# Three edits to an attention and expert-routing kernel: registers read a block ahead, gate steps spread, turned keys written at once

## What is computed

```python
xn = layernorm(x)
# attention: 16 heads of 128 + 64 rotary columns, latents of 128
c_Q, c_KV = xn @ W_DQ.T, xn @ W_DKV.T
k_R = rope(xn @ W_KR.T)                      # 64 columns, one for all heads
scores = clip(q @ k.T, -80, 80), causal; attn = softmax(scores / sqrt(192)) @ v
# experts: a shared one for every token, and the best 3 of 7 by a biased gate
p = softmax(xn @ gate_w + gate_b); chosen = top_k(p + biases, 3)
ffn(x, w1, wg, w2) = (silu(x @ w1) * (x @ wg)) @ w2
out = x + attention(xn) + ffn(xn, shared) + sum_e share_e * ffn(xn, expert e)
```

## Time and profile before

| | before |
|---|---|
| median of 3 runs | 1353.98 us (1353.33 to 1354.11) |
| the profiled execution's own time | 1354.13 us |
| its span, first to last instruction | 1352.40 us |
| TensorE products / weight loads | 97% / 80% of the span |
| VectorE / ScalarE / GpSimd | 55% / 46% / 47% |
| mean granted clock of TensorE | 0.997 |

### The profile page before, as it was taken

The page is one execution under the profiler, slowest core; times in us unless marked ns, Lnnn a source line. Parts: engine busy times, 40 slices in busy tenths (PEclk is TensorE's granted clock), DMA queues, the critical chain, the costliest instruction groups (busy, mean ns, idle before and its releaser), DMA issues.

```text
span 1352.4 us, 21141 instructions
## 1 busy us (share of the span) xinstructions
PE 1313.1 (97%) x6553; PEld 1085.1 (80%) x6553; DVE 741.2 (55%) x1365; ACT 620.2 (46%) x1146; POOL 629.5 (47%) x534
## 2 busy tenths in 40 slices
PE   5999999999999999999998999999999999999998
PEld 3778888778888888888886788888888888888887
DVE  6361165232222222222224678888888888788876
ACT  6421143222222222222225566666676667667664
POOL 5125584994060003200001476677666776676553
PEclk9999999999999999999999899999999999999999
DMA  8125552664241213311115124323242323322012
GB/s 274 54 106 199 191 182 77 184 185 133 64 148 56 63 53 105 108 50 62 59 37 179 39 46 79 76 44 82 39 92 46 72 62 64 76 40 61 17 47 95
DMA packets 72953, 123.25 MB, mean 91 GB/s; under 512 B 10960, under 2 KB 19280, under 8 KB 72848
## 3 DMA queue, kind: packets, MB, share of 16 engines
q1 hardware_dynamic: 42000, 60.49, 15.5%
q0 software_dynamic: 11312, 27.23, 9.3%
q10 hardware_dynamic: 19536, 34.17, 7.7%
HBM read 74.41 MB, written 39.05 MB: 84 GB/s over the span
## 4 chain that ended last, share of the span: by engine, by line
PE 88%; POOL 6%; DVE 2%; issue 1%; DMA 1%; ACT 1%; POOLq 0%; SPq 0%; ACTq 0%; DVEq 0%
PE bank L48 79%; PE bank L1648 4%; POOL slots L523 3%; PE bank L1440 2%; POOL slots L521 2%; PE bank L1381 1%; PE bank L1557 1%; DMA rows_b<-in_x 1%; PE bank L1367 0%; DMA rot_sin<-sum_b 0%; POOL slots L467 0%; DVE stats L886 0%; PE bank L1501 0%; POOL store_a L529 0%; POOLq L523 0%
## 5 line engine op out<-in xcount | busy, mean ns | idle before, releaser
L48 PE MATMUL bank<-store_b,store_a 128*128 128x512 f32 (+1 forms) x1536 | 324.6, 363 | 6.7 <-DVE store_b L1249 3.2
L48 PE MATMUL bank<-slots,x_turned 128*128 x1296 | 324.2, 399 | 6.1 <-POOL slots L523 3.9
L48 PEld LDWEIGHTS bank<-store_b,store_a 128*128 128x128 f32 x1536 | 255.0, 190 | 60.3 <-issue 8.7
L48 PEld LDWEIGHTS bank<-slots,x_turned 128*128 128x128 f32 x1296 | 235.8, 188 | 66.9 <-issue 22.9
L932 DVE TENSOR_TENSOR hid_t<-bank,hid_t 128x512 fp32r<-128x512 f32 x70 | 48.4, 691 | 357.7 <-ACT hid_t L651 357.7
L48 PE MATMUL bank<-slots,hid_t 128*128 (+1 forms) x840 | 208.6, 397 | 3.4 <-DVE hid_t L932 3.4
L48 PEld LDWEIGHTS bank<-slots,hid_t 128*128 128x128 f32 x840 | 153.5, 188 | 34.8 <-DVE hid_t L932 2.1
L48 PE MATMUL bank<-store_b 128*128 128x512 f32 x768 | 179.4, 389 | 0.0
L48 PEld LDWEIGHTS bank<-store_b 128*128 128x128 f32 x768 | 144.1, 188 | 29.9
L521 POOL CAST slots<-staging 128x512 f32 (+1 forms) x84 | 51.5, 613 | 182.0 <-PE bank L48 180.2
L825 ACT ACTIVATE p_store<-bank 128x512 f32<-128x512 f32 x160 | 95.6, 598 | 85.9 <-PE bank L48 84.4
(11 more groups left out here) (204 smaller groups left out, 1825.3 us busy)
## 6 DMA issues: line engine op xcount, KB each, us to landing
staging<-in_w SPq DMA_DIRECT2D x56, 256.0 KB, 2.8
sorted_y<-y_store ACTq DMA_DIRECT2D x54, 256.0 KB
rows<-sorted_x ACTq DMA_DIRECT2D x51, 260.0 KB, 2.7
rot_sin<-sum_b SPq DMA_DIRECT2D x128, 64.0 KB, 2.0
staging<-in_wg SPq DMA_DIRECT2D x28, 256.0 KB, 2.8
shared_y<-y_store ACTq DMA_DIRECT2D x16, 256.0 KB
raw<-in_wot SPq DMA_DIRECT2D x16, 256.0 KB, 2.8
acc<-in_x SPq DMA_DIRECT2D x16, 256.0 KB, 5.4
```

The lines of the kernel that those rows point to most:

```text
L48: made = pe.matmul(out, a, b, start=first and n == 0, stop=last and n == len(pairs) - 1, skip_group_check=onto)
```

## The change

The registers of a routed block are read by a function of its own, `find_job`. For block 16 it is called behind the projections and ahead of `up`; for the others in the block before, behind the row transposes and ahead of `down`. The wait on `job_low` stays in `up`. The 16 last steps of the gate are drawn in three portions (six after block 5's `multiply`, five before block 6's, the rest after it) and not all after block 5's. The two additions of the turned keys become one with twice the columns, whose inputs are read twice by a broadcast.

```diff
@@ projections, VectorE @@
-                dve.tensor_tensor(kr[:, i, 0, :], kr_cos[:, i, :], kr_sin[:, i, :], ALU.add)
-                dve.tensor_tensor(kr[:, i, 1, :], kr_cos[:, i, :], kr_sin[:, i, :], ALU.add).then_inc(on["kr_done"], 1)
+                cosine, sine = (v[:, i, :].unsqueeze(1).broadcast_to([P, 2, DR]) for v in (kr_cos, kr_sin))
+                dve.tensor_tensor(kr[:, i], cosine, sine, ALU.add).then_inc(on["kr_done"], 1)
@@ block loop, VectorE @@
-                if b in (4, 5):
-                    for _ in range(3 if b == 4 else 10):
+                if b in (4, 5, 6):
+                    for _ in range({4: 3, 5: 10, 6: 5}[b]):
                         next(gate, None)
                 multiply(b)
...
                 if b == 5:
+                    for _ in range(6):
+                        next(gate, None)
+                if b == 6:
                     for _ in gate:
                         pass
@@ TensorE @@
-            def job_ready(b):
+            def find_job(b):
...
-                made = pe.value_load(block_tab[0:1, r, 0:1], min_val=CH, max_val=CH * NE)
+                made_by[b] = pe.value_load(block_tab[0:1, r, 0:1], min_val=CH, max_val=CH * NE)
                 at_slot[b] = nc.values_load(block_tab[0:1, r, 1:2], engines=PE_ONLY, min_val=0, max_val=SLOT,
                                             skip_runtime_bounds_check_because="made on the chip from comparisons")
-                pe.wait_ge(on["job_low"], made)
...
@@ up @@
-                    job_ready(b)
+                    pe.wait_ge(on["job_low"], made_by[b])
@@ block loop, TensorE @@
                 if b == NT:
                     projections()
+                    find_job(NT)
                 up(b)
...
                 if NT + 1 < b + 1 < NBK:
                     turn_block(b + 1 - NT)
+                if NT <= b < NBK - 1:
+                    find_job(b + 1)
                 if b and b != NT:
                     down(b - 1)
```

More of the change, by code:

```diff
@@ L1389, in tokens @@
                 return x_turned[b % 2][:, 0], x_turned[b % 2][:, 1]
-            at_slot = {}
+            at_slot, made_by = {}, {}
             def weights(b, k):
```

## The result

| | before | changed |
|---|---|---|
| median | 1353.65 us | 1335.88 us (1334.69 to 1336.61) |
| ratio | | 0.9866, interval 0.9851 to 0.9881 |
| span of the profiled execution | 1352.40 us | 1334.80 us |

A forecast was written before the change was run, and what follows sets the result against it. TensorE, busy for 97% of the span, was taken as the bound, with time won only where it stands still. Savings of 6.2 + 1.2 + 0.7 + 5.2 + 1.9 + 1.2 = 16.4 us gave 1337.7 us, range 1334.2 to 1343.0.

The forecast's parts named there:

- Ordinary blocks: Blocks 26 to 69: gap before `up` closes, period 9.272 to 9.12 us; 6.2 us saved, bounds 4.5 and 6.5.
- The discount of 0.3 us for longer gaps: Ordinary blocks: 6.2 taken, not 6.5 us; some gaps (0.36 us and more) weren't explained by the register loads' duration alone.
- The place ahead of `down`: Moved register work ahead of `down(b-1)` costs nothing, as the sequencer is there 3.2 us before `down`.
- Blocks 16 and 17: Block 16's `up` starts 0.29 us behind L910, 1.2 us saved; the gap before block 17's `up` goes, 0.7 us.
- Blocks 18 to 25: Gaps where GpSimd holds L918 shrink, 0.1 to 0.2 us left in six; 5.2 us saved, bounds 3.0 and 5.8.
- Rival 1: Meetings with GpSimd fall badly in projections and blocks 18 to 25, savings there 0 and 3.0: 1341.1 us; chance 0.14.
- The gate's steps: `hid_low(5)` runs earlier, so TensorE's 2.07 us gap before `down(5)` goes; 1.9 us saved, bounds 1.7 and 1.9.
- Turned keys: Projections: one addition is held once by GpSimd where two are held twice; 1.2 us saved, bounds 0 and 2.8.
- rival 4: Attention's clock: the 16 us shift moves, drops or doubles a fall costing 3.4 us, 1334.3 or 1341.1 us; chance 0.10.
- Rival 2: L910's semaphore and travel, not register work, end last before `up`; the 6.2 us stay unsaved: 1346.5 us; chance 0.05.
- rival 5: The sequencer's lead is otherwise used, so only the gate's and keys' parts are saved: 1351.0 us; chance 0.03.
- rival 3: Register loads before `down` stop the sequencer until TensorE's queue is empty, 1.0 us in 53 blocks: 1390.7 us; chance 0.03.

The follow-up runs named there:

- registers alone: Kernel before with only `find_job` and its calls, gate steps and key additions as before: 1338.92 us, ratio 0.9887.
- behind down: Changed kernel with the registers of block b+1 read behind `down(b-1)`, directly ahead of `up(b+1)`: 1336.14 us, ratio 0.9864.
- new place twice: Changed kernel with added register work in `find_job` (loads written twice, 1.6 us of work in all): 1337.74 us, ratio 0.9878.
- after scale behind: Changed kernel with `row_low` ahead of `scale` in all three places: 1335.44 us, ratio 0.9858.
- Keys alone: Kernel before with only the one addition in place of two for the turned keys: 1353.35 us, ratio 0.9995.
- split late: Kernel before with GpSimd's first split of expert weights put behind the projections' turns: 1374.29 us, one run.
- gate alone: Kernel before with only the gate's last steps spread over two blocks: 1352.88 us, ratio 0.9987.
- scale behind: Kernel before with VectorE's two `scale` operations put behind the low half L910 in routed blocks from 18 on: 1349.17 us, ratio 0.9966.
- new place six: Changed kernel with five more rounds of register loads written into `find_job` (seven loads a block ran, 4.2 us): 1403.5 us, one run.

## Why the prediction was right, point by point

**Ordinary blocks** (6.2 us, measured 7.23 from block 26 to 69). The mechanism is shown: 0.65 us of added work costs its full length at the old place and nothing at the new one. The period came out at 391.49 / 43 = 9.104 us where the sum had 9.12. Four kernels with the work moved (registers alone, behind down, new place twice, after scale behind) have the same 391.49: with no wait left, the stage takes exactly what is queued. 7.23 us is more than the upper bound of 6.5, since 43 periods shorter by 0.016 us are 0.7 us. The discount of 0.3 us for longer gaps was wrong as well. They came mainly from a pause between the second load and the next sequencer entry, 0.09 to 0.21 us in every second block and 0.06 in the others; it is hidden with the rest. Keys alone and split late have the same pauses, nearly all in the same blocks and of the same length, gate alone and scale behind have none. What makes them no run shows.

**The place ahead of `down`** (nothing). Right; its limit, a lead of about 3.2 us, was measured as 3.3.

**Blocks 16 and 17** (1.2 and 0.7 us, measured 1.41 and 0.91). For 1.41: from the last turn's weight load to that of block 16 it was 2.09 us and is 0.68. I had priced the way from L910's end to the first weight load at 0.29 us, from the 0.25 us behind the second register load. It is less:

```profile
307.68 1.22 DVE L918 TENSOR_TENSOR row_share<-rows,owner 128x8 f32<-128x8 f32 x1
...
309.01 0.68 DVE L910 TENSOR_TENSOR x_turned<-bank,x_turned 128x512 fp32r<-128x512 f32 x1
309.83 1.77 PEld L48 LDWEIGHTS bank<-slots,x_turned 128*128 128x128 f32 x8
```

L910 ends at 309.69 and `up` of block 27 loads at 309.83, 0.14 us later. The other waits of `up` can be taken while the sequencer stands waiting, and then only one address step is left. Block 16 has 0.13 us as well.

**Blocks 18 to 25** (5.2 us, measured 5.98). The same rows show the worst meeting with GpSimd in the changed kernel: L918 held for 1.22 us and yet no gap. The 0.1 to 0.2 us that I left in six such gaps were that mis-sized 0.29. Rival 1 fell for this stage: the meetings go on, they only no longer reach TensorE. For the projections it was live, as gate alone showed (3.2 us of idle time instead of 2.8).

**The gate's steps** (1.9 us, measured 2.0: the 1.70 us up to block 15 and 0.28 by which the first product of this execution came later; 1.9 in gate alone). In the changed kernel, VectorE and `down(5)`, each in order of time:

```profile
92.19 0.69 DVE L932 TENSOR_TENSOR hid_t<-bank,hid_t 128x512 fp32r<-128x512 f32 x1 [2.15 <-ACT hid_t L651]
92.79 0.19 DVE L1138 CAST job_tab<-small 128x7 int32<-128x7 f32 x1
95.80 0.68 DVE L927 TENSOR_TENSOR hidden<-bank,hidden 128x512 f32<-128x512 f32 x1
...
98.23 0.36 DVE L1170 CAST block_tab<-block_f 128x54 int32<-128x54 f32 x1
...
93.83 2.68 PEld L48 LDWEIGHTS bank<-slots,hid_t 128*128 128x128 f32 x12
```

`hid_low(5)` ran at 92.19 and no longer at 94.88; it now waits for ScalarE and not for the gate, and `down(5)` has no idle time before it. The last step ends at 98.6 against a forecast of 98.4, and GpSimd begins to split at 178.0, sooner than before, so the later tables cost nothing:

```profile
L521 POOL CAST slots<-staging x84: 604/612/723, 178.0 to 533.0; 128x512 f32 x72, 128x512 fp32r<-128x512 f32 x12
```

**Turned keys** (1.2 us, measured 1.8, which is the 3.17 us saved from block 15 to 16 less block 16's 1.41). The additions and the turns behind them:

```profile
L948 DVE TENSOR_TENSOR kr<-kr_cos,kr_sin x16: 291/294/1115, 177.8 to 213.7; 128x128 f32<-128x128 f32 x16
L1503 PEld LDWEIGHTS bank<-ident,c 128*128 128x128 f32 x15 | 2.1, 140 | 1.1 <-issue 1.1
```

One addition takes 0.29 us alone and up to 1.12 us held; the idle time falls from 2.8 to 1.1 us. I took little because the meetings shift; in the seven profiles with the single addition the idle time was 1.0 to 1.6 us. The Trainium skill (SBUF — State Buffer, who interferes with whom) lets a VectorE instruction with two SBUF inputs contend with a GpSimd instruction that reads SBUF, and the later of the two waits; by that a tile with one addition can be held once and not twice. The trace agrees. Before, nine of the 32 additions were held, in seven of the tiles, and in two tiles both of the pair. Now seven of the 16 are, one of them by only 0.04 us. But five of the seven tiles had a single hold before too. Beyond the additions' own time the holds fell from 5.3 to 3.1 us in all, and how much of that is merging and how much is meetings that fell otherwise isn't separated.

**The sum.** The parts gave 19.3 us and not 16.4, and all six were priced too low. All but the keys came out above their upper bounds: 7.23 against 6.5, 5.98 against 5.8, 2.0 against 1.9, and 2.32 against 1.9 for blocks 16 and 17. Against that the start took 0.28 us longer, and attention 1.38 us. So the mechanisms were right and the terms cautious, and that the total came within 1.8 us of the forecast is in part luck. The profile has the granted clock at the lower of its two levels three times in the changed kernel's attention, 3.4 us each, and once for 6.8 us before. One of the new falls, with its stretch:

```profile
1185.00:1200.00 15.00, 14.73 (x74) 12.29 (x73) 11.99 (x19) 7.48 (x14) 9.22 (x6) 0.89 0.25 36
```

Over the profiles of this study the attention stage took 638.9 us with one such fall, 640.2 to 643.1 with two or with one of double length, and 642.6 to 643.3 with three, or with one of each length. The groups overlap (new place twice has two falls and 643.1 us), so the falls account for a part of the differences only. That is rival 4 in a weaker form: what follows the shift can cost or give a microsecond or two. Between blocks 16 and 69 the changed kernel has no fall. Three others have one at block 16 (it begins between 214 and 221 us), within or just behind an idle time of TensorE of 2.65, 3.8 and 23.4 us. Which idle time leads to a fall no run here isolates.

Rival 2 fell with registers alone, rival 5 with all of it. Of rival 3 the mechanism is real, as new place six showed, and at 0.95 us of work it is out of reach.

**Additive or not.** Alone the three edits gave 15.3, 1.4 and 0.9 us by their medians, 17.6 together; the change gives 17.8. The sum fits, but the parts need not be independent: in the one profile of keys alone its 1.6 us were lost again in the routed blocks, and with the registers moved too (registers alone against the change) 1.7 us from block 15 to 16 are kept.

## What to carry to other kernels

TensorE's sequencer does its own work in program order, and work that stands behind a wait starts only when the wait ends (here 0.04 us behind L910's end). Reads of registers, address arithmetic and assertions belong ahead of the last wait before the engine's queue runs out; here one wait earlier was enough, and a place is free as long as the queued work covers it. When a small gap repeats under "issue", look for what the sequencer does in it before looking for a late engine.

A tiny operation in the way of a critical one costs what it can be held for, not what it takes. Putting such operations behind the critical one is worth the hold, and merging two of them up to one hold; whether it is worth anything in the end depends on the slack of the stage behind.

## What was not expected of the hardware

- Once the sequencer stands ready at the last wait, 0.13 to 0.14 us pass from the end of the operation waited for to the next weight load; with the register work behind the wait it had been 1.24 us.
- Of the five kernels with two register loads behind the wait, gate alone and scale behind pause for 0.06 us behind the second load in every block, and the other three for 0.09 to 0.21 us in every second one. That is 1.2 us in all, as much as the gate's or the keys' edit alone gives in the median (1.4 and 0.9).
- The sequencer's lead over the array didn't grow with the time that it had to spare: behind the row transposes it was 3.3 us in the kernel before, in the changed one and with seven loads a block, with 16 products and their weight loads still to run. In the changed kernel its address steps just ahead of that point come 0.23 and 0.45 us apart, the time of one and of two products, and no longer 0.12 us.
- GpSimd's hold on an 8-column product of VectorE reached 1.22 us in the changed kernel too, 8 times its own 0.16 us, while the 512-column subtraction with one operand in PSUM took no more than 0.69 us in any profile, also where it began inside that GpSimd instruction.
